# A selective scan on one core: half of dt is made inside the scan, the B, C, dt product runs on two column halves, and the gate tiles go behind the first scan inputs

## The reference, cut to what matters

```python
xz = jnp.einsum('bld,ed->ble', xn, in_proj_w)
x_inner, z = jnp.split(xz, 2, axis=-1)
...
xc = _silu(jnp.transpose(xc, (0, 2, 1)))          # after a causal convolution of 4 taps
x_ssm = jnp.einsum('bld,ed->ble', xc, x_proj_w)    # 16 columns B, 16 columns C, 1 column dt
dt = jax.nn.softplus(x_ssm[..., -1:] * dt_w[:, 0] + dt_b)
A = -jnp.exp(A_log)
def step(h, inp):
    dt_t, B_t, C_t, u_t = inp
    dA = jnp.exp(dt_t[..., None] * A)
    h = dA * h + (dt_t * u_t)[..., None] * B_t[:, None, :]
    y_t = jnp.sum(h * C_t[:, None, :], axis=-1) + D_param * u_t
    return (h, y_t)
...
y = y * _silu(z)
```

## Time and profile before

| what | value |
|---|---|
| time, median of 3 runs | 859.79 us (851.26 to 860.62) |
| the profiled execution | 856.85 us, span 854.6 us |
| PE busy | 694.7 us (81%) |
| DVE busy | 673.3 us (79%) |
| ACT busy | 529.8 us (62%) |
| POOL busy | 497.3 us (58%) |

### The profile page before, as it was taken

The page is one execution under the profiler, slowest core; times in us unless marked ns, Lnnn a source line. Parts: engine busy times, 40 slices in busy tenths (PEclk is TensorE's granted clock), DMA queues, the critical chain, the costliest instruction groups (busy, mean ns, idle before and its releaser), DMA issues. The chain is left out here.

```text
span 854.6 us, 22547 instructions
## 1 busy us (share of the span) xinstructions
PE 694.7 (81%) x8285; PEld 522.1 (61%) x8285; DVE 673.3 (79%) x1498; ACT 529.8 (62%) x1439; POOL 497.3 (58%) x528
## 2 busy tenths in 40 slices
PE   4899999999999989369999708988889988851464
PEld 3578888888888776158899503345555555441333
DVE  6767778898888976667788557789889998679867
ACT  2644555566555655236676595579899787019296
POOL 2057777777777875045555176118899898424211
PEclk9999999999999999669999858999999999975778
DMA  7827000000000410027775533032333332010001
GB/s 295 279 94 301 1 2 2 7 1 8 1 8 8 161 51 14 7 69 217 225 201 147 120 115 89 2 100 78 102 101 127 103 108 96 3 49 0 1 13 38
DMA packets 30347, 71.44 MB, mean 84 GB/s; under 512 B 5472, under 2 KB 19488, under 8 KB 28320
## 3 DMA queue, kind: packets, MB, share of 16 engines
q1 hardware_dynamic: 25680, 57.54, 19.3%
q0 software_dynamic: 4560, 12.46, 6.1%
HBM read 59.57 MB, written 10.42 MB: 82 GB/s over the span
## 5 line engine op out<-in xcount | busy, mean ns | idle before, releaser
L1911 POOL TENSOR_TENSOR arena<-arena 128x1024 f32<-128x1024 f32 x63 | 147.2, 2385 | 29.1 <-DVE arena L1850 23.5
L1850 DVE TENSOR_TENSOR_SCAN arena<-arena,ps 128x1024 f32<-128x1024 f32 x64 | 141.8, 2270 | 14.1 <-ACT arena L1720 6.9
L1537 PEld LDWEIGHTS ps<-arena 64*64 64x64 f32 x4096 | 79.6, 134 | 63.9 <-DVE arena L1850 25.5
L1537 PE MATMUL ps<-arena 64*64 64x64 f32 x4096 | 92.0, 223 | 17.9 <-issue 8.9
L647 PE MATMUL ps<-arena 128*128 128x128 f32 (+1 forms) x768 | 101.2, 282 | 0.9 <-PEq L376 0.9
L647 PEld LDWEIGHTS ps<-arena 128*128 128x128 f32 (+1 forms) x768 | 91.7, 193 | 14.1 <-issue 12.9
L852 ACT ACTIVATE arena<-arena 128x128 f32<-128x128 f32 x256 | 98.8, 390 | 1.2 <-DVE arena L776 1.1
L1088 POOL DMA_INDIRECT arena<-tokens,arena x63 | 60.8, 965 | 59.6 <-PE ps L1124 42.4
L860 ACT ACTIVATE arena<-ps 128x512 f32<-128x512 f32 x64 | 38.2, 597 | 86.6 <-PE ps L666 86.6
L907 POOL TENSOR_TENSOR arena<-arena 128x512 f32<-128x512 f32 x64 | 66.7, 1043 | 21.5 <-DVE arena L782 21.5
L897 POOL TENSOR_TENSOR arena<-arena 128x256 f32<-128x256 f32 x64 | 47.9, 748 | 46.2 <-DVE arena L762 46.2
(11 more groups left out here) (326 smaller groups left out, 1522.1 us busy)
## 6 DMA issues: line engine op xcount, KB each, us to landing
arena<-c_rows SPq DMA_DIRECT2D x32, 512.0 KB, 3.7
arena<-in_E_gu SPq DMA_DIRECT2D x8, 1024.0 KB, 12.9
expert_out<-arena SPq DMA_DIRECT2D x63, 128.0 KB
arena<-in_E_dn SPq DMA_DIRECT2D x1, 4096.0 KB, 13.3
arena<-in_ctxT SPq DMA_DIRECT2D x2, 1024.0 KB, 5.1
arena<-in_A_o SPq DMA_DIRECT2D x1, 2048.0 KB, 16.6
arena<-in_X_o SPq DMA_DIRECT2D x1, 2048.0 KB, 23.7
arena<-in_F_w SPq DMA_DIRECT2D x4, 512.0 KB, 5.2
```

The source lines that it names most:

```text
L1537: t = eng.matmul(psD[d][cols, k, at:at + R], dtuT[rows, b, c, cols], diagB[rows, i % 2, b, :], start=True, stop=True)
L1850: eng.tensor_tensor_scan(hst[s % 4], dA[s % 4], psD[s % 2].rearrange("p k m -> p (k m)"), 0.0, ALU.mult, ALU.add).then_inc(h_ready, 1)
L1911: eng.tensor_tensor(hC[s % 4], hst[s % 4], Csb[i % 4], ALU.mult).then_inc(hC_ready, 1)
```

## The change

Six things are moved or split.

1. Ahead of the scan, dt and dt * xc are made for groups 0 and 1 only. The exponentials of groups 2 and 3 stand on ACT after decay(5), as one instruction of 1024 columns each, and their Ln after decay(7). Their `dt_and_dtu` stand on DVE after scan(9) and scan(12), their transposes on PE at s = 12 and 15, into the half of the scan's own PSUM that is free then (`TURN_AT`), and the copies back on ACT after decay(14) and decay(18). dBu(13) and dBu(16) wait for those copies.
2. `bc_dt` multiplies each 128 x 512 tile as two halves of 256 columns, into different output partitions (0 to 32 and 64 to 96) of one bank. `bc_rows` copies the two halves with two instructions.
3. On PE, gate tiles 6 and 7 go behind dBu(2) and dBu(3), each waiting for `z_copied`. All six late gate tiles are now copied by ACT; the three DVE copies are gone. decay(0) goes ahead of the first copies, the rest stand between decays 0 and 3.
4. `bc_rows(0)` and `dt_rows(0)` go ahead of the second half's projections, `bc_rows(1)` ahead of the first exponential on ACT.
5. On DVE the convolution conv(2, 0) goes ahead of the last `combine`. The projections of half 1 run in the order 0, 3, 1, 2.
6. SP issues the first two C loads without waiting for the gate tiles.

```diff
-        Z_FIRST, Z_MOVED, Z_COPIED = 2, 3, 3
+        Z_FIRST, Z_LATE = 2, 2 * CT - 2
-        Z_BANK = (5, 6, 4, 5, 6, 2, 3, 7)
+        Z_BANK = (5, 6, 6, 7, 2, 3, 2, 3)
-        XC_ORDER = ((0, 3, 1, 2), (0, 1, 2, 3))
+        XC_ORDER = ((0, 1, 3, 2), (0, 1, 2, 3))
+        XI_ORDER = ((0, 1, 2, 3), (0, 3, 1, 2))
+        TURN_BANK = (4, 0)
+        TURN_AT = {12: 2, 15: 3}
...
                             eng.wait_ge(xc_ready, CT * k + n + 1)
-                            t = eng.matmul(ps[0:E + 1, PROJ_BANK[k], :], w_bc[:, c, :], half(xc[:, c], k),
-                                           start=n == 0, stop=n == CT - 1)
+                            for q in range(2):
+                                t = eng.matmul(ps[q * R:q * R + E + 1, PROJ_BANK[k], 0:2 * P], w_bc[:, c, :],
+                                               quarter(xc[:, c], 2 * k + q), start=n == 0, stop=n == CT - 1)
...
-                for n in range(Z_FIRST, 2 * CT):
-                    if n == 2 * CT - 1:
-                        eng.wait_ge(btok_ready, 1)
+                for n in range(Z_FIRST, Z_FIRST + 4):
                     gate_rows(n)
-                eng.wait_ge(abs_ready, 2 * CT)
+                eng.wait_ge(btok_ready, 1)
+                turn_dtu(0, TURN_BANK[0])
+                dBu(0)
                 eng.wait_ge(zz_ready, 2 * CT)
-                turn_dtu(0)
+                turn_dtu(1, TURN_BANK[1])
                 eng.wait_ge(z_copied, 2)
-                turn_dtu(1)
-                eng.wait_ge(z_moved, Z_MOVED)
-                dBu(0)
-                turn_dtu(2)
-                eng.wait_ge(z_copied, Z_COPIED)
                 dBu(1)
-                turn_dtu(3)
                 for s in range(SLOTS + 2):
+                    if s in TURN_AT:
+                        eng.wait_ge(h_ready, s)
+                        turn_dtu(TURN_AT[s], 4 + 2 * ((s + 1) % 2))
                     if 0 < s < SLOTS - 1:
                         dBu(s + 1)
+                    if s in (1, 2):
+                        eng.wait_ge(z_copied, s + 2)
+                        gate_rows(Z_FIRST + 3 + s)
...
-                eng.wait_ge(exp_ready, 2 * CT)
-                for c in range(CT):
+                def logarithm(c):
+                    eng.wait_ge(exp_ready, 4 if c < 2 else c + 3)
                     eng.activation(dtu[:, c], dtu[:, c], ACT.Ln, bias=1.0).then_inc(ln_dt, 1)
+                logarithm(0)
+                logarithm(1)
...
+                decay(0)
+                turned_dtu(0, TURN_BANK[0])
+                gate_copy(Z_FIRST)
+                gate_copy(Z_FIRST + 1)
+                turned_dtu(1, TURN_BANK[1])
                 decay(1)
-                turned_dtu(2)
+                gate_copy(Z_FIRST + 2)
+                gate_copy(Z_FIRST + 3)
                 decay(2)
-                turned_dtu(3)
+                gate_copy(Z_FIRST + 4)
                 scaled(2)
+                gate_copy(Z_FIRST + 5)
                 decay(3)
                 for i in range(2, 2 * ST):
                     decay(2 * i)
+                    for s in TURN_AT:
+                        if s + 2 + s % 2 == 2 * i:
+                            turned_dtu(TURN_AT[s], 4 + 2 * ((s + 1) % 2))
                     if i + 1 < 2 * ST:
                         scaled(i + 1)
                     decay(2 * i + 1)
+                    if i == 2:
+                        for c in range(2, CT):
+                            eng.wait_ge(abs_ready, CT + c + 1)
+                            eng.activation(dtu[:, c], dtu[:, c], ACT.Exp, scale=-1.0).then_inc(exp_ready, 1)
+                    if i == 3:
+                        logarithm(2)
+                        logarithm(3)
...
-                for c in range(CT):
-                    dt_and_dtu(c)
+                dt_and_dtu(0)
+                dt_and_dtu(1)
                 eng.wait_ge(c_stored, 32)
                 for s in range(SLOTS):
                     scan(s)
+                    if s in (9, 12):
+                        dt_and_dtu(2 + s // 12)
```

More of the change, by code:

```diff
@@ L1654, in bc_rows @@
                     eng.wait_ge(proj_done, k + 1)
-                    eng.activation(half(bcf[0:E + 1], k), ps[0:E + 1, PROJ_BANK[k], :],
-                                   ACT.Copy).then_inc(bcf_ready, 1)
+                    for q in range(2):
+                        t = eng.activation(quarter(bcf[0:E + 1], 2 * k + q), ps[q * R:q * R + E + 1, PROJ_BANK[k], 0:2 * P],
+                                           ACT.Copy)
+                    t.then_inc(bcf_ready, 1)
                 def exponentials(k, first=0, end=CT):
@@ L1829, in _ @@
                 conv(1, 0)
+                conv(2, 0)
                 combine(HB + 3)
@@ L1833, in _ @@
                 scales_out(eng, cs, 1)
-                conv(2, 0)
                 for c in range(CT - 1):
@@ L1840, in _ @@
                 steps(1)
-                for n in range(Z_FIRST, Z_FIRST + Z_MOVED):
-                    k, m = Z_TILES[n]
-                    eng.wait_ge(z_done, n + 1)
-                    eng.tensor_copy(half(zs[:, m], k), ps[:, Z_BANK[n], :]).then_inc(z_moved, 1)
                 def scan(s):
```

54 lines of the change are left out of this document (24 added, 30 removed).

## The result

The changed kernel took 874.5 us, the median of four runs (872.16 to 875.18), against 857.25 us for four runs of the kernel before: 1.0202 times the time, with a 95% interval of 1.0169 to 1.0236. The forecast was 873 us, with a range of 862 to 880. The agreement is closer than the working deserves: the forecast loss of 13.8 us stood on the median of the runs known then, 859.8, and the measured loss is 17.3 us. So the sum was 3.5 us short, and its base 2.5 us high: that the two nearly cancel is luck.

A forecast was written before the change was run, and what follows sets the result against it. Ahead of the scan a chain from engine to engine was taken to bound the kernel, in the scan DVE. Eight terms summed to +13.8 us on 859.8, giving 873.6, rounded to 873 us; range for 8 in 10, 862 to 880.

The forecast's parts named there:

- (a): Start of the scan: only groups 0 and 1 are waited for, so scan(0) starts earlier, -6.7 us.
- (b): scan(1): PE's second transpose now stands behind dBu(0), so scan(1) follows scan(0) later, +1.5 us.
- (c): scan(3): two gate tiles in PE's queue and their copies ahead of decay(3) on ACT, +3.0 us.
- (d): scan(4) to scan(9): exponentials, Ln and two table loads join ACT's run without idle time, +5.5 us.
- (e): dt_and_dtu for groups 2 and 3 on DVE between scans, counted at their whole time, +4.9 us.
- (h): scan(9) to scan(16): new waits hide half of the 4.1 us of waits the kernel had anyway, -2.1 us.
- (f): The four moved DVE instructions beside POOL's multiply: 1.7 us lost for one instruction of each pair, +3.4 us.
- third rival: All four moved DVE instructions stand behind a whole POOL multiply, 9.6 us instead of 3.4, so 880 us; chance 0.10.
- (g): scan(16): dBu(16) waits for ACT's copy of group 3's transpose, queued behind other ACT work, +4.3 us.
- The rest only moves: The rest of the scan and what follows keep the same spacing, from slot 20 on about 14 us later.
- POOL never set the pace: Second rival: POOL sets the scan's pace, DVE delays cost nothing, the earlier start is kept whole, 853 us; chance 0.07.
- the halves ran beside each other: Fourth rival claimed the opposite: column halves don't run side by side, steps(1) up to 1.8 us later, 875 us; chance 0.05.

The follow-up runs named there:

- e3: The changed kernel with group 3's transpose on PE one slot earlier, at s = 14 instead of 15; 870.08 us, ratio 1.0155 to the kernel before.
- e6: The changed kernel without the four DVE instructions between the scans, so the second half computes other values; 868.14 us, ratio 1.0152 to the kernel before.
- e2: The changed kernel with exponentials and Ln of groups 2 and 3 ahead of the scan again; 875.27 us, ratio 1.0192 to the kernel before.
- e9: The changed kernel with the four moved DVE instructions one by one, behind scans 9, 10, 12 and 13; ratio 1.0190 to the kernel before.
- e11: The changed kernel run again, unaltered, as the measure for the last group of runs; ratio 1.0213 to the kernel before.
- e8: The kernel before with the column halves of bc_dt and bc_rows alone; ratio 0.9995 to the kernel before.
- e10: The kernel before with the column halves and ACT's copy of the second half's rows ahead of the exponentials; ratio 0.9984 to the kernel before.

## Why the prediction was right, and which of its terms were off

(a) The start: -7.1 (-6.9 counted from the bias matmuls) for a forecast of -6.7, out of two errors. steps(1) started 1.8 us earlier, near the bound of 2.0 rather than the 0.2 taken; from dt_and_dtu to scan(0) it took 7.4 us instead of 6.3, because dBu(0) ran at half clock. With the clock whole (e3) that path is 6.5.

(b) and (c): +3.2 and +3.6, where +1.5 and +3.0 were forecast. The mechanisms were right: with the clock whole, scan(3) comes 11.62 us after scan(0) (e3, e6), and the terms gave 3.75 + 7.9 = 11.65. What was mis-sized is the price of one dBu and one transpose on PE, taken from rows at the full clock; at half it was 2.4 us more.

(d) +5.6, forecast +5.5, shown by e2: exponentials, Ln and two loads took 1.99 + 2.00 + 2 x 1.28 = 6.55 us without idle time on either side, and the waits for ACT are ahead of scans 6 to 9, as named, 6.0 us instead of 4 to 5. The Trainium skill (ScalarE: Activation LUTs, "What ACT_TABLE_LOAD costs") adds a drain of about 1380 ns to each load; here the Ln starts 10 ns after its load ends, so the measurement decides, and the sum was right to leave the drain out.

(e) to (h), scans 9 to 16: +10.2, forecast 4.9 + 3.4 + 4.3 - 2.1 = +10.5. The parts differ. The port (f) took 2.05 us once, not 1.7 twice, and it is the order of issue that decides (e9). The Trainium skill (SBUF - State Buffer, "Who interferes with whom") says that whoever issues first holds the shared ports for its whole instruction: e9 agrees from both sides, 0.9 us for POOL when DVE is first, and for the fourth instruction, which starts inside a multiply, a wait to its end. In the changed kernel DVE lost 2.05 behind POOL. The third rival took the lock as certain for all four; it needs POOL to be ahead and working. (e) was counted in full, but e6 shows that its second half covers a wait that would be there anyway. (g) was a wait of 5.6 us ahead of scan(16), forecast 4.3; a slot earlier, e3 saves 1.9 of it.

(h) and the rest. "The rest only moves" did not hold in the profile: slots 16 to 63 took 4.0 us more, so the last scan came 19.4 us later and not about 14. In e11 it is +2.4, and in e3, with the same work from slot 16 on, nothing (115.91). So these 4.0 us are no fixed price of the moved work. The pauses of PE which the prediction let the new waits hide are not bound to slots 9 to 16: e8 and e10 run these slots 3.8 us faster than the kernel before and lose 2.9 and 3.4 us behind slot 16. In all three PE has 7 to 10 us of such pauses in the scan, at other places. What sets the places is not settled. Neither is how much of the 4.0 they make; in the changed kernel 6.8 us at half clock, from 650.6 us on, lie there too.

Rivals: POOL never set the pace (no wait of a scan is put down to it), the halves ran beside each other (1.92 us for 3.62), and of the new costs only the second pair of DVE instructions fell together with a wait (e6).

In one sum: starting 7.1 us earlier is no gain of that size, since 4.9 of it is DVE's own work, moved into the scan. What was won ahead is some 2 us; what was moved met ACT without slack, PE between a dBu and its scan, and POOL's port.
